# Latent attention rewritten: steps of two heads by 256 queries, queries projected straight into turned form

## The reference

```
q = (x @ wq).reshape(b, s, H, QH);  q_nope, q_pe = q[..., :128], q[..., 128:]     # QH = 128 + 64
ckv = rmsnorm(x @ wkv_a[:, :64]) * scale;  k_pe = x @ wkv_a[:, 64:]
q_pe, k_pe = rope(q_pe), rope(k_pe)          # (x1*cos - x2*sin, x2*cos + x1*sin), halves of 32
scores = (q_nope . k_nope + q_pe . k_pe) * QH**-0.5, causal;  attn = softmax(scores)
out = (attn @ v) over 16 heads of 128, @ wo
```

## Time and profile before

| | us |
|---|---|
| median of 3 runs | 1471.77 (1463.14 to 1471.78) |
| the profiled execution's own time | 1471.49 |
| its span, from the first to the last instruction | 1469.1 |
| busy in the span: PE / DVE / POOL / ACT | 1278.5 / 973.3 / 826.6 / 655.6 |
| first attention phase, 490.7 to 897.3 | 406.6 |
| second attention phase, 941.6 to 1347.8 | 406.2 |

### The profile page before, as it was taken

How to read it: one execution, slowest core, us unless ns; L and a number is a source line. 1 busy time by engine, 2 the same in 40 slices (tenths; PEclk the granted TensorE clock), 3 DMA queues, 4 the chain that set the end, 5 groups by cost and what they waited for, 6 DMA issues and landing times. The chain is left out here.

```text
span 1469.1 us, 23884 instructions
## 1 busy us (share of the span) xinstructions
PE 1278.5 (87%) x7096; PEld 966.7 (66%) x7097; DVE 973.3 (66%) x2055; ACT 655.6 (45%) x1183; POOL 826.6 (56%) x654
## 2 busy tenths in 40 slices
PE   6974699999983599999999997789999999998797
PEld 5863455555552477777677776767777777777686
DVE  4568522222224859888778886868888888976657
ACT  3221233333320356655555654246565655665242
POOL 2026778888874355555555556445555555555554
PEclk9976799999995899999999999999999999999999
DMA  9358245555554000000000000000000000002001
GB/s 326 115 159 214 90 65 82 80 81 79 81 72 133 15 1 9 8 7 0 8 7 0 1 1 12 8 8 8 8 0 7 7 7 0 0 1 60 5 8 51
DMA packets 66218, 67.13 MB, mean 46 GB/s; under 512 B 15040, under 2 KB 59648, under 8 KB 66016
## 3 DMA queue, kind: packets, MB, share of 16 engines
q1 hardware_dynamic: 48048, 42.38, 9.8%
q0 software_dynamic: 15168, 20.72, 9.1%
q10 hardware_dynamic: 2928, 3.15, 0.7%
HBM read 45.12 MB, written 21.10 MB: 45 GB/s over the span
## 5 line engine op out<-in xcount | busy, mean ns | idle before, releaser
L1525 POOL TENSOR_TENSOR att_prob_lo<-att_prob,att_prob_hi 128x896 fp32r<-128x896 f32 (+1 forms) x192 | 383.6, 1998 | 194.9 <-ACT att_prob_hi L1472 194.9
L1386 PE MATMUL all_bank<-att_q_hl,sequence_k_hl 128*128 128x512 f32 (+2 forms) x1152 | 282.5, 354 | 5.8 <-DVE att_minus L1593 5.7
L1578 DVE TENSOR_REDUCE att_peak<-all_bank 128x1 f32<-128x512 f32 (+3 forms) x384 | 207.6, 549 | 72.5 <-PE all_bank L1373 54.3
L1406 PE MATMUL all_bank<-att_prob_hi,sequence_v_hl 128*128 128x512 f32 (+2 forms) x768 | 231.1, 384 | 7.5 <-ACT late_oT L1481 7.4
L1465 ACT ACTIVATE att_prob<-all_bank 128x896 f32<-128x896 f32 (+1 forms) x192 | 162.8, 848 | 148.4 <-PE all_bank L1392 147.8
L1386 PEld LDWEIGHTS all_bank<-att_q_hl,sequence_k_hl 128*128 128x128 f32 x1152 | 193.1, 191 | 24.9 <-DVE att_minus L1593 7.1
L1370 PE MATMUL all_bank<-sequence_k_hl,att_q_hl 128*128 128x512 f32 (+3 forms) x384 | 168.3, 441 | 11.1 <-DVE att_peak L1578 10.9
L1472 ACT CAST att_prob_hi<-att_prob 128x896 fp32r<-128x896 f32 (+1 forms) x192 | 168.6, 878 | 2.5
L1519 POOL TENSOR_TENSOR att_rows<-att_by_cos,att_by_sin 128x128 f32<-128x128 f32 x128 | 58.6, 458 | 182.9 <-DVE att_by_sin L1564 182.9
L903 PE MATMUL all_bank<-early_w_gu,moe_xgT 128*128 x316 | 148.8, 553 | 3.6 <-issue 2.4
L868 POOL DMA_INDIRECT sums<-moe_y,early_slot_far x79 | 125.4, 1587 | 36.4 <-issue 18.8
(11 more groups left out here) (246 smaller groups left out, 2288.0 us busy)
## 6 DMA issues: line engine op xcount, KB each, us to landing
sequence_w_raw<-wqk_rows SPq DMA_DIRECT2D x16, 256.0 KB, 2.7
early_w_gu<-in_gate SPq DMA_DIRECT2D x16, 224.0 KB, 5.9
early_w_gu<-in_up SPq DMA_DIRECT2D x16, 224.0 KB, 6.1
early_w_down<-in_down SPq DMA_DIRECT2D x1, 3584.0 KB, 19.8
sums<-early_zero SPq DMA_DIRECT2D x18, 128.0 KB, 3.5
all_xT<-in_xT SPq DMA_DIRECT2D x4, 512.0 KB, 8.7
all_x_tok<-in_x SPq DMA_DIRECT2D x1, 2048.0 KB, 16.8
x_rows<-all_x_tok SPq DMA_DIRECT2D x4, 512.0 KB, 3.0
```

What stands on the lines that cost most here:

```text
L1386: nc.tensor.matmul(ps, k_hl[:, ks, j * P:(j + 1) * P], q_hl[r // 2 % 2][:, qs, r % 2, q0:q0 + w], start=n == 0, stop=False)
L1406: mm = nc.tensor.matmul(pv_ps[:, q0 - qc * WIDE:WIDE], v_hl[:, vs, j, :], part[:, x % 3, a:z], start=j == 0 and n == 0, stop=last and n == 2)
L1525: nc.gpsimd.tensor_tensor(prob_lo[:, x % 3, a:z], prob[:, x % 2, a:z], prob_hi[:, x % 3, a:z].bitcast(F32), ALU.subtract).then_inc(lo_sb, 1)
L1578: nc.vector.tensor_reduce(peak[:, r % 2, n, i:i + 1], max_ps[y % 2][:, 0:w], AX_X, ALU.max).then_inc(peak_sb, 1)
```

## The change

It leaves the other phases nearly as they are and rewrites `phase_attention`. The names of parts stay: `scores`, `probs`, `highs`, `low`, `values`, `sums`, `peaks`, `spread`, `divide`.

- **Queries already turned.** `query` uses the weights as the stationary operand and 512 tokens as the moving one, so the result has query rows on the partitions: 4 chunks of a pair (2 heads by 2 halves of the sequence), 6 matmuls of 512 columns each. No copy to rows, no transposes. Tables of cosine and sine in turned form (1 MB) are a new input, loaded in the phase before.
- **Rotation.** VectorE makes all products, from PSUM: two of 32 partitions by 512 with the sine (L1546), one of 128 by 512 with the cosine (L1549), with a table of ones for the rows that do not turn. GpSimd adds them (`rotate`, L1493), ScalarE writes the high part (`q_high`), GpSimd the low part (`q_low`, L1500), which VectorE made before.
- **Steps.** A pair has 10 steps: 4 blocks of 256 queries, both heads side by side in 512 columns, against pairs of key tiles up to the diagonal. A block's values go to banks 4 and 5 in turn.
- **Side work.** Queries and maximum pieces of the next pair share banks 6 and 7 in turn, in the order that `aside` gives; a matmul there waits until VectorE is done with the item two places before (`bank_free`).
- **Divisions** come a whole block at a time (`DIVIDE_AT`): two reciprocals, then two products. The last pair's last block, two halves, is left to `phase_output`.
- Everything is written out, without loops; the table of constants is loaded in two parts.

```diff
-                def divide(u, r, qc, n):
...
-                    nc.vector.reciprocal(rden[:, n % 2, :], den[qc][:, n * P:(n + 1) * P]).then_inc(rden_sb, 1)
-                    by_pair(dve, rden_sb, u, r, k, done + 1)
-                    nc.vector.tensor_tensor(own, own, rden[:, n % 2, :], ALU.mult).then_inc(o_sb, 1)
...
+    NEXT_PIECES = [0, 0, 1, 2, 3, 3, 3, 3, 3, 3]
+    OWN_PIECES = [2, 1] + [0] * (NG - 2)
+    FIRST_PIECES = [3, 3, 2] + [0] * (NG - 3)
+    EARLY = NP - sum(FIRST_PIECES)
+    DIVIDE_AT = {2: 0, 4: 1, 7: 2, 1: 3}
...
+    def aside(n, x):
+        left = NP - sum(FIRST_PIECES if n == 0 else OWN_PIECES)
+        own = FIRST_PIECES if n == 0 else OWN_PIECES
+        out = [("query", n + 1, x)] if n + 1 < PAIRS and x < QC else []
+        out += [("piece", n, left + sum(own[:x]) + a) for a in range(own[x])]
+        if n + 1 < PAIRS:
+            out += [("piece", n + 1, sum(NEXT_PIECES[:x]) + a) for a in range(NEXT_PIECES[x])]
+        return out
...
+                def bank_free(item):
+                    a = place[item]
+                    if a < 2:
+                        return
+                    kind, n, v = order[a - 2]
+                    if kind == "query":
+                        pe.wait_ge(sin_sb, n * QC + v + 1)
+                    else:
+                        pe.wait_ge(peak_sb, n * NP + v + 1)
...
+                def query(item):
+                    _, n, k = item
+                    h, c = chunk(k)
+                    bank_free(item)
+                    if n:
+                        pe.wait_ge(w_sb, n)
+                    i = 0
+                    for xs, ws in ((0, 0), (0, 1), (1, 0)):
+                        for kc in range(KC):
+                            mm = nc.tensor.matmul(bank_of(item), w_hl[:, ws, kc, h * P:(h + 1) * P],
+                                                  x_hl[:, xs, kc, c * WIDE:(c + 1) * WIDE],
+                                                  start=i == 0, stop=i == 3 * KC - 1)
+                            i += 1
+                    mm.then_inc(q_mm, 1)
...
+                for u in range(STEPS):
+                    n, x, _, _ = at(u)
+                    beside_it = aside(n, x)
+                    ahead = u + AHEAD < STEPS
+                    if ahead:
+                        scores(u + AHEAD, 0)
+                    for item in beside_it[0:1]:
+                        beside(item)
+                    if ahead:
+                        scores(u + AHEAD, 1)
+                    for item in beside_it[1:2]:
+                        beside(item)
+                    values(u, 0)
+                    for item in beside_it[2:3]:
+                        beside(item)
+                    values(u, 1)
+                    for item in beside_it[3:]:
+                        beside(item)
...
+                def rotate(n, k):
+                    c = n * QC + k
+                    own = swapped[:, c % 2]
+                    pool.wait_ge(sin_sb, c + 1)
+                    nc.gpsimd.tensor_tensor(raw[:, c % 2], raw[:, c % 2], own, ALU.add).then_inc(rot_sb, 1)
+                def q_low(n, k):
+                    c = n * QC + k
+                    h, half = chunk(k)
+                    own = q_hl[n % 2][:, :, h, half * WIDE:(half + 1) * WIDE]
+                    pool.wait_ge(q_hi_sb, c + 1)
+                    nc.gpsimd.tensor_tensor(own[:, 1], raw[:, c % 2], own[:, 0].bitcast(F32), ALU.subtract
+                                            ).then_inc(q_lo_sb, 1)
...
+                def rope(n, k):
+                    c = n * QC + k
+                    cols = slice(chunk(k)[1] * WIDE, (chunk(k)[1] + 1) * WIDE)
+                    ps = bank_of(("query", n, k))
+                    dve.wait_ge(q_mm, c + 1)
+                    if c >= 2:
+                        dve.wait_ge(rot_sb, c - 1)
+                    for i, o in ((LORA + 32, LORA), (LORA, LORA + 32)):
+                        nc.vector.tensor_tensor(swapped[o:o + 32, c % 2], ps[i:i + 32], sin[i:i + 32, cols], ALU.mult)
+                    if c >= 2:
+                        dve.wait_ge(q_lo_sb, c - 1)
+                    nc.vector.tensor_tensor(raw[:, c % 2], ps, cos[:, cols], ALU.mult).then_inc(sin_sb, 1)
...
+                def divide(n, i):
+                    e = n * NB + i
+                    dve.wait_ge(sums_sb, e + 1)
+                    for half in range(2):
+                        if e:
+                            dve.wait_ge(o_sb, 2 * (e - 1) + half + 1)
+                        nc.vector.reciprocal(rden[:, half, :], den[:, e % 2, half * P:(half + 1) * P]).then_inc(rden_sb, 1)
+                    for half in range(2):
+                        own = oT[:, n, i * BW + half * P:i * BW + (half + 1) * P]
+                        dve.wait_ge(rden_sb, 2 * e + half + 1)
+                        nc.vector.tensor_tensor(own, own, rden[:, half, :], ALU.mult).then_inc(o_sb, 1)
...
+                for u in range(STEPS):
+                    n, x, _, _ = at(u)
+                    items = aside(n, x)
+                    if items and items[0][0] == "query":
+                        items[0:2] = items[1::-1]
+                    for item in items:
+                        beside(item)
+                    if x in DIVIDE_AT:
+                        i = DIVIDE_AT[x]
+                        if i < NB - 1:
+                            divide(n, i)
+                        elif n:
+                            divide(n - 1, i)
+                    if x == 5 and n + 2 < PAIRS:
+                        weights_high(n + 2)
+                    if x == 6 and n + 2 < PAIRS:
+                        weights_low(n + 2)
```

More of the change, by code:

```diff
@@ L1235, in phase_attention @@
+        whole = m.sb("whole", [P, 2, NB, 2, 2])
+        minus = m.sb("minus", [P, NB, WIDE], BF16)
         prob = m.sb("prob", [P, 2, 2 * WIDE])
@@ L1263, in phase_attention @@
-        pieces_of = lambda i: [y for y in range(NP) if pieces[y][0] == i]
-        LOW = 4
-        CHUNKS = S // WIDE
-        AHEAD = 2
-        HEADS = 4
-        ROUNDS = H // HEADS
-        PIECES_AT = [(0, 1, 2), (3, 4, 5), (6, 7), (8, 9), (10, 11), ()]
-        QUARTERS = WIDE // P
-        def span(group):
-            qc, tiles = group
-            end = (qc + 1) * WIDE
-            a, z = WIDE - (end - tiles[0][1]), WIDE + end - tiles[1][1]
-            return a, z, [(a, WIDE), (WIDE, z)]
@@ L1282, in by_head @@
-        def by_head(engine, sem, u, r, k, more):
-            engine.wait_ge(sem, u * (HEADS * k) + (r * k + more + 2 * k))
-        def by_pair(engine, sem, u, r, k, more):
-            engine.wait_ge(sem, u * (HEADS // 2 * k) + (r * k + more + 2 * k))
-        def rounds(engine, step, peel_first=False):
-            def steps(u, last):
-                for r in range(HEADS):
-                    for x in range(NG):
-                        more = not (last and r == HEADS - 1)
-                        step(u, r, x, more, PIECES_AT[x] if more else (), *made_at(r, x, last))
-            if peel_first:
-                steps(0, False)
-            with engine.Fori(int(peel_first), ROUNDS - 1) as u:
-                steps(u, False)
-            steps(ROUNDS - 1, True)
@@ L1322, in phase_attention, with bank_of, chunk @@
+        aside_ps = [bank[:, n, :] for n in (6, 7)]
+        def bank_of(item):
+            return aside_ps[place[item] % 2]
+        def chunk(k):
+            return k % 2, k // 2
         with nc.Block() as block:
@@ L1443, in _, with beside @@
-                turn(0, 1, 0)
-                scores(0, 0, 1, 1)
-                rounds(pe, step)
+                def beside(item):
+                    (query if item[0] == "query" else piece)(item)
+                for k in range(QC):
+                    query(("query", 0, k))
+                for y in range(8):
+                    piece(("piece", 0, y))
+                scores(0, 0)
+                scores(0, 1)
+                for y in range(8, EARLY):
+                    piece(("piece", 0, y))
@@ L1528, in step @@
-                def step(u, r, x, more, peak_pieces, made, turned):
-                    if made:
-                        rotated(u, *made)
-                    if x + AHEAD < NG:
-                        low(u, r, x + AHEAD)
-                    elif more:
-                        low(u, r + 1, x + AHEAD - NG)
-                for sem, n in ((rot_sb, QT), (lo_sb, NG)):
-                    pool.sem_inc(sem, 2 * n)
-                for t in range(QT):
-                    rotated(0, 0, t)
-                low(0, 0, 0)
@@ new lines, in low @@
+                def low(u):
+                    w = width(u)
+                    pool.wait_ge(hi_sb, u + 1)
+                    nc.gpsimd.tensor_tensor(prob_lo[:, u % 3, 0:w], prob[:, u % 2, 0:w],
+                                            prob_hi[:, u % 3, 0:w].bitcast(F32), ALU.subtract).then_inc(lo_sb, 1)
+                nc.gpsimd.memset(swapped, 0.0).then_inc(clear_sb, 1)
+                rotate(0, 0)
```

(22 more changed lines are left out.)

497 lines of the change are left out of this document (197 added, 300 removed).

## The result

The changed kernel takes 1603.04 us (median of 4 runs, 1600.15 to 1607.99), the kernel before 1471.7: a ratio of 1.091, 95% interval 1.086 to 1.096. The forecast was 1588 with the range 1518 to 1645. The profiled execution has a span of 1601.0 us, 1.8 less than its own time.

A forecast was written before the change was run, and what follows sets the result against it. It took PE as the bound, VectorE close behind. From a 1469.1 us span: +82 for longer pairs, +48 clock, -8 phase edges, -6 `phase_output`, giving 1585, plus 2.4 outside the span: forecast 1588 us, range 1518 to 1645.

The forecast's parts named there:

- second rival: A chunk's products on VectorE start without overlapping their neighbours: 19 us more on the loop, 1607 us; chance 0.17.
- The loop of a chunk: Steps 2 and 3: chunks follow each other at 7.7 us, as VectorE's division products wait for GpSimd.
- PE's waits: Waits of PE in a pair, mostly for VectorE: summed as 12.2 us, rounded up to 13.
- Step 0: VectorE takes the first own piece before the first query chunk, so PE waits 2.0 us.
- step 2's queries: They wait for chunk 1, behind a reduction, `whole` and `minus` on VectorE: 1.3 us of PE wait.
- the next query: From chunk 1's end to chunk 2's, PE has 4.8 us of work and waits 2.9.
- steps 4 to 6: Three pieces each and a further division: PE waits 1.4 us in step 4, about 1 for casting weights in 5 and 6.
- The second piece of step 3: It uses chunk 3's bank; from chunk 2's end to chunk 3's, PE waits 4.6 us.
- The clock: PE's clock halves once or twice a pair behind waits: 3 us a pair, +48 us, ends 0 and 6 a pair.
- The rival in which the clock holds: PE's waits are split by half scores and values, so the clock does not fall: 1540 us; chance 0.22.
- PE's own list: PE's matmuls in a pair, counted from the program: 42.0 us after the change, against 46.5 before.
- The faster rival: GpSimd doesn't hold the division's products up, so the chunk loop is 4.4 us, under PE's 4.8: 1386 us; chance 0.07.

The follow-up runs named there:

- e1_divisions_away: Changed kernel with a pair's four divisions moved from steps 2, 4, 7 and 1 to steps 4, 6, 8 and 0: 1543.4 us.
- e2_short_gpsimd: Changed kernel with GpSimd's rotation addition and queries' low part cut to 32 of 512 columns from each phase's third pair on: 1552.4 us.
- e10_one_product: Changed kernel with each division as one reciprocal and one product of 256 columns instead of two each of 128: 1567.7 us.
- e6_filler: Changed kernel plus eight useless matmuls of 256 columns ahead of each of a pair's third and fourth query chunks: 1605.2 us.
- e7_both: Changed kernel with divisions moved to steps 4, 6, 8 and 0, and VectorE taking the query chunk ahead of the own piece in step 0: 1460.8 us.
- e9_filler_more: Changed kernel plus 44 useless matmuls a pair, ahead of the third and fourth query chunks and step 3's second piece: 1577.2 us.
- e4_partition0: Changed kernel with a chunk's two 32-partition products at partition 0, written to scratch rows, leaving the rotation out: 1577.3 us.
- e8_best: Changed kernel with small work reordered: query chunks in steps 0, 1, 3, 4, single 256-column reciprocals and products steps apart, pieces moved: 1445.0 us, ratio 0.983 to the kernel before.

## Why the prediction was right

The mechanism is the one that the prediction gave, at the places that it gave, with one exception: the products of a chunk don't overlap, as its second rival said. The pairs are 59.0 us apart, a little over the 55 to 58 that it named. Step by step:

- **The loop of a chunk.** Laid out by hand as 7.7 us, measured 7.5. Two errors nearly cancel in it: a chunk's own products take 2.1 us instead of 1.9, as they don't overlap, and what stands between two chunks takes 5.4 instead of 5.8. It holds the two divisions' products behind `low` and then `q_low`. Shown by `e1_divisions_away`, `e2_short_gpsimd` and `e10_one_product`, which each take away a different part.
- **PE's waits**, forecast 13 a pair, are 10.3. (The items of the prediction add up to 13.2 and not to the 12.2 of its sum: the 1 us for casting the weights is missing there. Rounding up to 13 covered the slip.) Step 0 was put at 2.0 and has 2.23; step 2's queries at 1.3, 1.49; the next query at 2.9, 2.67; steps 4 to 6 at 2.4, about 1.2. The second piece of step 3, put at 4.6, has 2.77, because PE ran at a granted clock of 0.64 ahead of it (603.40 to 608.10) and came late. In `e6_filler`, where the clock is 1.00 there, it is 4.34. So 1.6 of what is missing here is found in the next term.
- **The clock**, forecast 3 a pair with the end 6, costs 48.7 - 43.7 = 5.0 of busy time by the same list in `e7_both`. Some 1.6 of it is hidden in the wait of step 3, so about 3.4 a pair reach the time, an estimate from the one pair shown. The rival in which the clock holds (1540) is refuted. `e9_filler_more`, 26 us faster with more work, shows that some of it is real cost behind the waits.
- **PE's own list** was the mis-sized term: 42.0 forecast, 43.7 measured. I took the distance between starts from two short rows and a line for the other lengths; the same sum gave 46.5 for the list before, against a busy time of 47.65, and I let that difference go as overlap. It was +27 us for 16 pairs.
- **The rival of products that don't overlap** (1607, chance 0.17) is true in its cause, and its 1607 is nearer to the 1603 measured than the 1588 of the forecast, whose sum takes the overlap for given. `e4_partition0` puts it at 0.30 us a chunk, the 19 us that it was priced at. A chance of 0.17 was too little: nothing in the rows spoke against it.
- **The faster rival** needed a GpSimd that is idle when the products come. It is busy in the loops shown; `e7_both` moves the products instead.
- **The rest.** The phases' edges gave 15 us instead of 8: the phases are 943.5 us for 16 pairs of 59.0, before 812.8 for 16 of 49.9. The 6 us in `phase_output` didn't come: outside the phases the kernel takes 1.2 us more. The window of that phase is 0.8 shorter.

Sum: 16 x (59.0 - 58.0) = +16, edges -7, the rest +7, together 16 us above the 1585 of the span, which is 1601. The near hit is in part luck: list +27 and clock +32 against waits -43. Some 25 us of the last two are only moved from the one to the other (1.6 a pair); without them it is list +27 and clock +7 against waits -18.

What the change itself is worth: its list is shorter by 47.65 - 43.7 = 4.0 us a pair, 63 us in all. The order in which the small work was laid down cost more than that: another order (`e8_best`) is 158 us faster than the changed kernel. Of the list's gain it keeps 27 us; no run recovered the other 36.
